# DLRM tower on one core: one-hot blocks moved from VectorE's compare to two ScalarE steps, the last sum's operand in PSUM

## The reference

```python
e = jnp.stack([tbl_f[ids[:, f]] for f in range(32)], axis=1)      # 2048 x 32 x 256
iu, ju = jnp.triu_indices(32, k=1)
z = jnp.einsum('bnd,bmd->bnm', e, e)[:, iu, ju]                   # 2048 x 496
h = jnp.concatenate([z, dense_ctx], axis=1)                       # 2048 x 512
h = jnp.maximum(h @ W_top1 + b_top1, 0.0)                         # 2048 x 512
h = jnp.maximum(h @ W_top2 + b_top2, 0.0)                         # 2048 x 256
y = h @ W_top3                                                    # 2048 x 1
```

## Time and profile before

| what | value |
|---|---|
| median of 3 runs | 636.33 us (635.46 to 636.99) |
| the profiled execution's own time | 639.15 us |
| its span in the trace | 637.1 us |
| granted TensorE clock, mean over the span | 0.941 |
| busy: TensorE / VectorE / ScalarE / GpSimd | 522.1 / 233.7 / 186.2 / 470.9 us |

### The profile page before, as it was taken

How to read it: one execution, slowest core, us unless ns; L and a number is a source line. 1 busy time by engine, 2 the same in 40 slices (tenths; PEclk the granted TensorE clock), 3 DMA queues, 4 the chain that set the end, 5 groups by cost and what they waited for, 6 DMA issues and landing times.

```text
span 637.1 us, 23971 instructions
## 1 busy us (share of the span) xinstructions
PE 522.1 (82%) x11105; PEld 472.1 (74%) x11105; DVE 233.7 (37%) x223; ACT 186.2 (29%) x337; POOL 470.9 (74%) x439
## 2 busy tenths in 40 slices
PE   0769999697996979789795988969797987989765
PEld 0768898686885868678685968868686877878654
DVE  2654163333433234424333343323443343241310
ACT  2432060514133051413304141230514133060512
POOL 7878777787877778777787777778777777777700
PEclk9985999899998989989899999979999998999887
DMA  8976342534335343343435333353434433333300
GB/s 197 237 218 182 96 117 87 134 85 118 93 94 131 93 121 93 98 117 98 109 94 128 99 98 113 97 131 94 121 91 105 114 95 110 103 106 111 106 6 2
DMA packets 31813, 70.79 MB, mean 111 GB/s; under 512 B 10465, under 2 KB 16753, under 8 KB 31089
## 3 DMA queue, kind: packets, MB, share of 16 engines
q0 software_dynamic: 20736, 56.65, 31.2%
q1 hardware_dynamic: 10978, 12.61, 9.3%
HBM read 69.22 MB, written 0.01 MB: 109 GB/s over the span
## 4 chain that ended last, share of the span: by engine, by line
PE 55%; POOL 19%; DMA 12%; issue 10%; ACT 3%; DVE 0%; ACTq 0%; DVEq 0%; POOLq 0%
PE look_ps L294 23%; POOL rows L249 19%; PE gram_ps L312 14%; DMA rows<-in_tbl,row_ids 12%; PE turn_ps L278 7%; PE top_ps L333 7%; PE top_ps L341 4%; ACT turned L393 2%; PE top_ps L324 1%; ACT products L419 0%; ACT turned L414 0%; ACT area L429 0%; DMA row_ids<-in_ids 0%; DVE products L499 0%; ACT area L445 0%
## 5 line engine op out<-in xcount | busy, mean ns | idle before, releaser
L249 POOL DMA_INDIRECT rows<-in_tbl,row_ids x432 | 470.1, 1088 | 132.4 <-issue 119.1
L294 PE MATMUL look_ps<-one_hot,small 125*128 125x256 f32 (+1 forms) x1344 | 205.1, 301 | 1.8 <-issue 1.2
L278 PE MATMUL turn_ps<-ident,rows 128*128 128x128 f32 x864 | 128.5, 291 | 87.3 <-DMA rows<-in_tbl,row_ids 86.6
L294 PEld LDWEIGHTS look_ps<-one_hot,small 125*128 125x128 f32 x1344 | 177.8, 199 | 7.5 <-issue 2.8
L278 PEld LDWEIGHTS turn_ps<-ident,rows 128*128 128x128 f32 x864 | 103.0, 149 | 99.8 <-DMA rows<-in_tbl,row_ids 79.9
L490 DVE COPY turned<-turn_ps 128x512 f32<-128x512 f32 (+1 forms) x112 | 100.2, 933 | 183.5 <-PE turn_ps L278 183.5
L507 DVE TENSOR_TENSOR one_hot<-ids_across,sub_row 125x2048 fp32r<-125x2048 int32 (+1 forms) x42 | 92.2, 2194 | 104.3 <-PE look_ps L294 93.9
L312 PE MATMUL gram_ps<-turned 128*32 128x31 f32 x8192 | 114.7, 200 | 12.2 <-issue 9.9
L312 PEld LDWEIGHTS gram_ps<-turned 128*32 128x32 f32 x8192 | 94.0, 111 | 36.0 <-issue 15.5
L402 ACT ACTIVATE ahead<-look_ps 128x512 f32<-128x512 f32 (+1 forms) x42 | 24.3, 578 | 289.9 <-PE look_ps L294 289.9
L393 ACT ACTIVATE turned<-turn_ps 128x512 f32<-128x512 f32 x112 | 72.6, 695 | 115.7 <-PE turn_ps L278 115.5
(11 more groups left out here) (21 smaller groups left out, 55.1 us busy)
## 6 DMA issues: line engine op xcount, KB each, us to landing
rows<-in_tbl,row_ids POOLq DMA_INDIRECT x432, 3.3
ids_across<-in_small_ids SPq DMA_DIRECT2D x38, 128.0 KB, 4.9
area<-in_tbl SPq DMA_DIRECT2D x3, 896.0 KB
w_sb<-in_tbl SPq DMA_DIRECT2D x2, 896.0 KB
w_sb<-in_W_top SPq DMA_DIRECT2D x4, 256.0 KB, 4.2
w_sb<-in_W_top SPq DMA_DIRECT2D x1, 512.0 KB, 7.7
area<-in_tbl SPq DMA_DIRECT2D x3, 104.0 KB
ids_across<-in_small_ids SPq DMA_DIRECT2D x4, 64.0 KB, 6.1
```

The lines of the kernel that those rows point to most:

```text
L249: pool.indirect_dma_start(out=rows[:, f, :], out_offset=None, in_=tables[SMALL + f], in_offset=bass.IndirectOffsetOnAxis(ap=row_ids[:, t, ...
L278: last = pe.transpose(turn_ps[n % RING][:, at:at + P], rows[:, f, c * P:(c + 1) * P], ident[:, :])
L294: last = pe.matmul(look_ps[:, c * width:(c + 1) * width], small[:, f, r, part, c * P:(c + 1) * P], one_hot[n % 2][:, r, 0:width], start=(r ...
```

## The change

VectorE's compare is gone. ScalarE makes the one-hot block in two steps instead. First it forms the distance |id - row number| with eight activations Abs, one for each r, with the bias `minus_rows[:, r]`, a number for each partition (125 x 256 each, or 125 x 128 for a one-tile lookup). Then one activation Relu over the whole block, with scale -1 and bias 1, turns the distance 0 into 1 and every greater one into 0. Eight increments of a new semaphore (`distance_made`) stand between the two steps. `make_one_hot(n + 1)` stands in ScalarE's queue ahead of `keep_looked_up(n)`. VectorE makes `minus_rows` once. In `last_layers` the biased layer 2 result (`hidden2`) is written to the second half of PSUM's `top_ps` and no longer to SBUF; the weighted sum reads it there and writes its products, which nobody reads, to SBUF (`weighted`). As `top_ps` is then in use for longer, `turn_features` waits for `y_done` instead of `h2_kept`. `last_layers` follows the turned copies directly in VectorE's queue.

```diff
-        hidden2 = area[:, 3 * FEATURES:3 * FEATURES + HIDDEN2]
+        hidden2 = top_ps[:, HIDDEN2:2 * HIDDEN2]
+        weighted = area[:, 3 * FEATURES:3 * FEATURES + HIDDEN2]
...
                 if t > 0:
-                    pe.wait_ge(h2_kept, t)
+                    pe.wait_ge(y_done, t)
...
+            def make_one_hot(n):
+
+                _, _, tiles = LOOKUPS[n]
+                width = tiles * P
+                act.wait_ge(ids_across_in[n % IDS_RING], n_ids(n))
+                if n >= 2:
+                    act.wait_ge(looked_up, n - 1)
+                for r in range(SUB):
+                    act.activation(one_hot[n % 2][:, r, 0:width], ids_across[0:SP, n % IDS_RING, 0:width], ACT.Abs,
+                                   bias=minus_rows[:, r:r + 1]).then_inc(distance_made, 1)
+                act.wait_ge(distance_made, (n + 1) * SUB)
+                act.activation(one_hot[n % 2][:, :, 0:width], one_hot[n % 2][:, :, 0:width], ACT.Relu,
+                               bias=1.0, scale=-1.0).then_inc(one_hot_made, 1)
...
             split_high(0)
+            act.wait_ge(minus_rows_ready, 1)
+            make_one_hot(0)
...
                     if n + 1 < SMALL:
                         split_high(n + 1)
+                    make_one_hot(n + 1)
                     keep_looked_up(n)
...
                 for n in range(FIRST[t], FIRST[t + 1]):
+                    if n + 1 < len(LOOKUPS):
+                        make_one_hot(n + 1)
                     keep_looked_up(n)
...
-            def make_one_hot(n):
-                _, _, tiles = LOOKUPS[n]
-                width = tiles * P
-                dve.wait_ge(ids_across_in[n % IDS_RING], n_ids(n))
-                if n >= 2:
-                    dve.wait_ge(looked_up, n - 1)
-                dve.tensor_tensor(
-                    one_hot[n % 2][:, :, 0:width],
-                    ids_across[0:SP, n % IDS_RING:n % IDS_RING + 1, 0:width].to_broadcast([SP, SUB, width]),
-                    sub_row[:, :].rearrange("p (r a) -> p r a", a=1).to_broadcast([SP, SUB, width]),
-                    ALU.is_equal).then_inc(one_hot_made, 1)
...
-                dve.scalar_tensor_tensor(out=hidden2, in0=hidden2, scalar=0.0, in1=w3_sb[:, :],
+                dve.scalar_tensor_tensor(out=weighted, in0=hidden2, scalar=0.0, in1=w3_sb[:, :],
                                          op0=ALU.max, op1=ALU.mult, accum_out=y_sb[:, t:t + 1]).then_inc(y_done, 1)
...
-            dve.wait_ge(sub_row_ready, 1)
-            make_one_hot(0)
+            dve.wait_ge(row_numbers_ready, 1)
+            dve.tensor_scalar(minus_rows[:, :], row_numbers[:, :], -1.0, None, ALU.mult).then_inc(minus_rows_ready, 1)
             split_low(0)
...
-                for k, n in enumerate(range(FIRST[t] + 1, FIRST[t + 1] + 1)):
-                    if n < len(LOOKUPS):
-                        make_one_hot(n)
-                    if k == 0 and t > 0:
-                        last_layers(t - 1)
-                if t == TILES - 1:
+                if t > 0:
                     last_layers(t - 1)
```

More of the change, by code:

```diff
@@ L104, in dlrm_tower @@
         ids_across = sbuf("ids_across", [P, IDS_RING, 2 * P], int32)
-        sub_row = sbuf("sub_row", [SP, SUB], int32)
+        row_numbers = sbuf("row_numbers", [SP, SUB], int32)
+        minus_rows = sbuf("minus_rows", [SP, SUB])
         one_hot = [sbuf(f"one_hot{i}", [SP, SUB, 2 * P], fp32r) for i in range(2)]
@@ L145, in dlrm_tower @@
         ident_ready = sem("ident_ready")
-        sub_row_ready = sem("sub_row_ready")
+        row_numbers_ready = sem("row_numbers_ready")
+        minus_rows_ready = sem("minus_rows_ready")
+        distance_made = sem("distance_made")
         high_ready = sem("high_ready")
@@ L257, in _ @@
                                base=0, pattern=[[-1, P]], channel_multiplier=1).then_inc(ident_ready, 1)
-            pool.iota(sub_row[:, :], pattern=[[1, SUB]], base=0, channel_multiplier=SUB).then_inc(sub_row_ready, 1)
+            pool.iota(row_numbers[:, :], pattern=[[1, SUB]], base=0,
+                      channel_multiplier=SUB).then_inc(row_numbers_ready, 1)
             for t in range(TILES):
@@ L536, in _ @@
                     n = LOOK_AFTER.index(i)
-                    make_one_hot(n + 1)
                     if n + 1 < SMALL:
```

## The result

| | before | changed |
|---|---|---|
| median | 636.66 us (4 runs, 635.46 to 638.48) | 585.14 us (4 runs, 583.86 to 586.61) |
| ratio | 1 | 0.919, 95% interval 0.916 to 0.922 |
| profiled execution: own time, span | 639.15, 637.1 us | 586.61, 584.6 us |

The median is 51.5 us lower: 585.14 us, where 583.4 was forecast.

What follows compares the result with a forecast made beforehand. GpSimd's queue of 432 gathers was taken as the bound. Span 637.1 - 46.2 - 6.7 = 584.2 us, then + 2.05 - 2.8 gave 583.4 us; forecast 579 to 588 us (70 in 100), range 577 to 592.

Steps and rivals of the forecast that it cites:

- The bound: GpSimd's gather queue sets the pace; without compares, tiles 2 to 15 take 378 x 1.25 = 472.5 us, gain 46.2 us.
- The start: Tiles 0 and 1: tile 2's first gather goes at 79 instead of 85.67, after a new TensorE wait; gain 6.7 us.
- ScalarE's block: Nine activations a lookup on ScalarE: 5.1 us a block, 3.3 us for one tile, 207 us in all.
- The spare time before the copies: In look phases with three lookups, gaps of 6.2 us or more hold a 5.1 us block, 1.1 us to spare.
- the steady state: Look phases: ScalarE's blocks fit beside TensorE's work and delay no copy; cost 0.
- the count: At the start, five more ScalarE blocks make the third lookup some 2 us later, hidden by TensorE's wait for rows.
- The operand in PSUM: Last layers' weighted sum with one operand in PSUM: 0 gain counted; at most 7 us if all sixteen held gathers.
- The tail: After the last gather: landing, last turn, pair products and three layers stay fixed at 33.0 us.
- the last step: From span to median: add 2.05 us for the execution's own time, subtract 2.8 us for the median.
- long instructions with two SBUF inputs: VectorE's 42 compares and 5 subtractions hold GpSimd's gathers up, 1.3 us each, 61 us in all.
- TensorE's waits for rows: TensorE's 86.6 us of waits shrink to some 35 us.

Runs made afterwards that it cites:

- e3: Kernel before, each VectorE compare replaced by eight tensor_scalar compares with one SBUF tensor input, ScalarE untouched: 586.35 us, ratio 0.917.
- e8: Changed kernel with the fifth lookup's ids loaded right behind the third table: 976.38 us on a slower chip, kernel before 931.98 there, ratio 1.055.
- e1: Kernel before with only the last weighted sum's operand moved to PSUM: 637.98 us against 639.03, ratio 0.998.
- e9: Kernel before with each VectorE compare cut into eight, still with two SBUF inputs each: 595.35 us, ratio 0.931.
- e5: Changed kernel plus an idle one-input VectorE compare at each of the 42 old places: 953.41 us on a slower chip, kernel before 931.98 there.
- e6: Changed kernel with each Abs done twice: 1007.17 us on a slower chip, kernel before 931.98 there.
- e7: Changed kernel without the last unit's gather in tiles 1 to 15: 949.93 us on a slower chip, kernel before 931.98 there.
- e11: Changed kernel with each Abs done twice, same edit as e6: 996.75 us on a second slower chip, kernel before 910.64 there.
- e12: Changed kernel without the last unit's gather in tiles 1 to 15, same edit as e7: 944.48 us on a second slower chip, kernel before 910.64.

## Why the prediction was right

*The bound.* GpSimd's queue set the pace, and it still does: a tile takes 33.8 us from tile 2 on (79.72 to the last start, 551.06, is 471.3 us for 377 gathers, 1.25 each). The forecast was 378 x 1.25. Gain there: 46.2 us predicted; measured, 603.17 - 85.67 less 551.06 - 79.72 is 46.2 us.

*The start.* Tile 2's first gather was put at 79, with a new wait for TensorE; it starts at 79.72 after a wait of 1.93. TensorE's turn phase begins 0.9 us earlier than before, at 78.84. Gain 5.9 us against 6.7 predicted. The five gathers beside the subtractions take 7.6 us more than five median ones, and 7 was the estimate. Part of GpSimd's wait is ScalarE's: in e3, where ScalarE makes no blocks, TensorE begins this turn phase 1.3 us earlier, at 77.57, and the gather's wait is 0.46 us.

*ScalarE's block.* 5.1 us predicted, 5.2 measured; the pitch of the Abs 0.37 us predicted, 0.40 measured. The spare time before the copies was put at 1.1 us; measured, it is never under 0.98 from tile 0's look phase on, and 1.0 to 2.0 in most phases with three lookups. Total added: 207 predicted, 205 measured. No cost in the steady state, as forecast. At the start the count missed one thing: the fifth block waited 2.8 us for its ids, and behind it TensorE's lookup waited 5.8 us for ScalarE's copy. Most of that wait is not ScalarE's doing, as e3 has one of 4.8 us at the same lookup.

```profile
47.38 2.44 ACT L463 ACTIVATE one_hot<-ids_across,minus_rows 125x128 fp32r<-125x128 int32 x8 [2.75 <-DMA ids_across<-in_small_ids]
...
51.33 7.06 PE L301 MATMUL look_ps<-one_hot,small 125*128 125x128 f32 x32 [5.81 <-ACT ahead L409]
```

What GpSimd's new wait would be without it is not shown: e8 was to measure that, and ran on a chip where GpSimd's queue is not the bound.

*The operand in PSUM.* Zero predicted from the row, no effect measured in e1 (ratio 0.998, 0.996 to 1.001). The number is right, but the row was misread. The gather in it begins at 283.49, 0.09 us before the sum, so it says nothing of a gather that begins inside one. In the trace of the kernel before only two do, 0.01 and 0.30 us after its start, neither at a point where the other runs show a hold-up. So the forecast of nothing was in part luck. The rule of the Trainium skill ("SBUF — State Buffer", Who interferes with whom), which the prediction set aside here, holds for this short instruction too, by the two pairs of lines under e9. What it costs is at most a quarter of a microsecond a time, as the instruction is short, and not 7 us in all. The prediction also took an instruction with one SBUF input for harmless without the exception for the mode with two ports, and e5's one-input instruction held gathers up.

*The tail.* 33.0 us behind the last gather predicted; 584.6 - 552.0 = 32.6 measured. The span was forecast at 584.2 us and is 584.6. Most of the 1.7 us between the two medians comes from the last step, in which the median was put 2.8 us below the profiled execution; it is 1.5 below.

*Where the reasoning was loose.* The prediction named "long instructions with two SBUF inputs" as the cause, where the rows could not tell the part of the inputs from that of the length. For this change both give the same time, so the number did not suffer; but a reader who took only "two inputs" from it would have overlooked that the compare could stay on VectorE, cut into eight (e9: 595 us), or in eight with one input (e3: 586 us). TensorE's waits for rows shrank to 43.5 us where 35 were forecast, as TensorE was busy for 505.2 us and not for 522.1, at a mean granted clock of 0.958 against 0.941.

## What to carry to other kernels

When an engine's instructions are sometimes twice as long as their median, look at what ran beside the long ones, before asking which engine is busiest: here a queue with 74% busy time was the bound, and a third engine set its pace. If GpSimd issues gathers, keep VectorE's instructions with two SBUF inputs short; cutting one 2.3 us instruction into eight got four fifths of the gain without moving any work. A PSUM operand instead of one of the two freed the gathers beside a 0.42 us instruction; a long instruction with two inputs, one of them in PSUM, was not run. Moving work to ScalarE got all of the gain, and ScalarE had a gap of 6.2 us or more at most places where 5.2 us were put. That a longer block costs time once the gap is full was argued, and not measured on a chip of the usual speed. Nor does the gain hold on every chip (last paragraph below).

## What the runs showed that was not expected

A gather that is held up ends 0.8 us after the end of VectorE's instruction, whichever it was. In the kernel before, 45 gathers beside VectorE's work take over 1.1 us, and each ends 0.81 to 0.82 us after the end of a compare or a subtraction. It was the same beside the faster one-input instruction of e5 (0.81 us in the lines shown), the short compares and the weighted sum. So the price of a hold-up can be worked out from where the gather begins: what is left of VectorE's instruction, less some 0.13 us.

An int32 to bf16 tensor_scalar with a constant ran at 1.2 us for 2048 elements, twice as fast as the two-input compare, and held gathers up all the same, for as long as it ran. A faster VectorE instruction is no protection for GpSimd's gathers.

On two chips the kernel before took 911 and 932 us, 43 and 46% more than on the others. In the traces from those chips TensorE stands idle in "issue" holes, mostly of up to 2.5 us (in e5's chain that ended last, "issue" is 35% of the span), at a mean granted clock of 0.745 to 0.756. There e6, e7, e8, e11 and e12, all with ScalarE's blocks, took 944 to 1007 us against 911 and 932 for the kernel before, with ratios of 1.026 to 1.094, so each of them lost; e5's runs (931 to 959 us) can't be told from the kernel before. The changed kernel itself was not run there. Why the variants lose in that condition stays open: GpSimd's queue does not set the pace there, as its long waits for TensorE show (322 us in e7), and no run isolates what does.
